# Attention on one core: sums of probabilities moved next to the value products, and one key block more summed by TensorE

## What is computed

```
att   = einsum('bhgqd,bhkd->bhgqk', qg, k) / sqrt(32)
att   = where(causal, att, -inf)
probs = softmax(att, axis=-1)
ctx   = einsum('bhgqk,bhkd->bhgqd', probs, v)
```

## Time and profile before

| | us |
|---|---|
| median of 3 runs | 2504.25 |
| the three runs | 2514.14, 2503.09, 2504.25 |
| span of the profiled execution | 2510.1 |
| that execution's own time: the one run that can contain this span | 2514.14 |
| attention, steady groups 1 to 30 | 664 to 1697 |
| most groups, scores of unit 0 to scores of unit 0 | 33.9 |

### The profile page before, as it was taken

How to read it: one execution, slowest core, us unless ns; L and a number is a source line. 1 busy time by engine, 2 the same in 40 slices (tenths; PEclk the granted TensorE clock), 3 DMA queues, 4 the chain that set the end, 5 groups by cost and what they waited for, 6 DMA issues and landing times. The chain is left out here.

```text
span 2510.1 us, 36950 instructions
## 1 busy us (share of the span) xinstructions
PE 2433.2 (97%) x13716; PEld 1678.6 (67%) x13716; DVE 1698.5 (68%) x2878; ACT 1046.8 (42%) x1873; POOL 1650.9 (66%) x865
## 2 busy tenths in 40 slices
PE   5999999999999999999999999998999999999998
PEld 3788888887555555555555555554688788888886
DVE  4766666677888887888878888873655354455553
ACT  3433333331666666666666666665211111111111
POOL 3743333341798998999989999993755455555543
PEclk9999999999999999999999999999999999999999
DMA  6532333351535325344233334312433333333330
GB/s 229 201 118 85 115 113 116 122 155 72 161 99 145 73 66 160 82 114 108 66 89 82 82 94 137 82 48 93 134 97 96 100 94 101 110 93 100 110 93 25
DMA packets 179727, 267.49 MB, mean 107 GB/s; under 512 B 20508, under 2 KB 113884, under 8 KB 178400
## 3 DMA queue, kind: packets, MB, share of 16 engines
q1 hardware_dynamic: 179552, 265.13, 36.0%
HBM read 183.22 MB, written 80.81 MB: 105 GB/s over the span
## 5 line engine op out<-in xcount | busy, mean ns | idle before, releaser
L1072 POOL TENSOR_TENSOR p_sum<-p_sum,p_ring 128x1024 f32<-128x1024 f32 (+2 forms) x465 | 991.4, 2159 | 81.0 <-PE ctx_ps L1133 59.7
L263 DVE TENSOR_REDUCE neg_max<-scores_q 128x1 f32<-128x512 f32 (+1 forms) x1168 | 708.7, 655 | 124.0 <-PE scores_q L250 66.0
L966 ACT ACTIVATE p_ring<-scores 128x512 f32<-128x512 f32 (+1 forms) x896 | 453.0, 565 | 243.1 <-DVE scores L1020 178.6
L250 PE MATMUL scores_q<-k_stack,q_stack 96*128 96x512 f32 (+1 forms) x1473 | 442.6, 380 | 3.0 <-DVE neg_max L263 2.0
L1112 PE MATMUL scores<-q_stack,k_stack 98*128 98x512 f32 (+1 forms) x1216 | 423.6, 425 | 12.3 <-ACT p_ring L966 8.8
L617 POOL TENSOR_TENSOR roped_hilo<-roped_hilo 128x512 fp32r<-128x512 f32 x80 | 105.8, 1322 | 339.7 <-ACT roped_hilo L459 339.7
L1112 PEld LDWEIGHTS scores<-q_stack,k_stack 98*128 98x128 f32 x1216 | 198.4, 192 | 175.4 <-ACT p_ring L966 93.2
L250 PEld LDWEIGHTS scores_q<-k_stack,q_stack 96*128 96x128 f32 x1473 | 266.2, 192 | 71.2 <-DVE neg_max L263 36.3
L666 PE MATMUL proj_ps<-h_hi,w_hi 128*128 128x512 f32 x752 | 300.3, 399 | 0.7 <-POOL w_lo L606 0.7
L666 PE MATMUL proj_ps<-h_hi,w_lo 128*128 128x512 f32 x752 | 294.3, 391 | 0.0
L666 PE MATMUL proj_ps<-h_lo,w_hi 128*128 128x512 f32 x752 | 293.6, 390 | 0.0
(11 more groups left out here) (178 smaller groups left out, 3709.9 us busy)
## 6 DMA issues: line engine op xcount, KB each, us to landing
q_stack<-qk_t SPq DMA_DIRECT2D x96, 512.0 KB, 6.9
qk_t<-roped_hilo SPq DMA_DIRECT2D x80, 512.0 KB, 2.8
x_in<-in_L_attn_resid SPq DMA_DIRECT2D x32, 512.0 KB, 6.3
ctx_t<-ctx_raw SPq DMA_DIRECT2D x64, 256.0 KB, 5.6
prefetched<-in_L_wmod SPq DMA_DIRECT2D x4, 4096.0 KB, 13.3
prefetched<-ctx_t SPq DMA_DIRECT2D x31, 512.0 KB, 4.1
prefetched<-inv_t SPq DMA_DIRECT2D x124, 128.0 KB, 5.5
k_stack<-qk_t SPq DMA_DIRECT2D x96, 128.0 KB, 8.8
```

What stands on the lines that cost most here:

```text
L250: last = nc.tensor.matmul(dst[:, a, :], qs[0:MHI, h, i * P:(i + 1) * P], ks[0:MHI, lo:lo + w], start=not first and (a == 0 or not diag), s ...
L263: nc.vector.tensor_reduce(sh.negm[:, lo // HALF, hs[0]:hs[-1] + 1, i:i + 1], src, AX.X, ALU.max, negate=True).then_inc(sh.s_mx.sem, 1)
L966: nc.scalar.activation(p[:, a * per:(a + 1) * per, :], src[:, a * per:(a + 1) * per, :], ACT.Exp, scale=SM_SCALE).then_inc(s_ex.sem, 1)
L1072: nc.gpsimd.tensor_tensor(a, a, probs(n, u), ALU.add).then_inc(s_ap.sem, 1)
```

## The change

TAIL_FROM takes unit 18 (key block 6 of the second half) out of GpSimd's list and into the sums product: GpSimd makes 14 additions a group, and the step "sum" of the second half has four more products, of 256 columns each, from the ring. SUM_AT puts the sums of the second half in tick 11 and those of the first in tick 15, where they stand ahead of the value products of the same tick. INV_AT moves the three steps of the inversion from ticks 9, 12 and 15 to 12, 15 and 18. SUM_AT_LAST is as it was.

```diff
-TAIL_FROM = {0: 4, 1: 7}
+TAIL_FROM = {0: 4, 1: 6}
...
-SUM_AT = {1: 9, 0: 16}
+SUM_AT = {1: 11, 0: 15}
 SUM_AT_LAST = {1: 6, 0: 12}
 AHEAD = 5
 TURN_AT = 17
-INV_AT = (9, 12, 15)
+INV_AT = (12, 15, 18)
```

## The result

| | before | after |
|---|---|---|
| median | 2505.1 us (14 runs) | 2511.84 us (14 runs) |
| lowest to highest | 2501.16 to 2514.14 | 2509.37 to 2514.61 |
| ratio of the times | | 1.0024, interval 1.0015 to 1.0032 |
| span of the profiled execution | 2510.1 | 2509.1 (its own time 2510.94) |

The medians differ by 6.7 us, and the ratio puts the cost at 0.24% (0.15 to 0.32%), clear of no change. The forecast from the median was +6 us.

What follows compares the result with a forecast made beforehand. The prediction took TensorE's instruction order as the bound, with two places on VectorE's time, not GpSimd. Terms +7.5 + 4.7 - 2 - 4 = +6 us gave 2510 us from the median 2504.25; range 2494 to 2530.

Steps and rivals of the forecast that it cites:

- sums of the second half with block 6: Ticks 8 to 11: moved sums with four added products cost +0.25 us a group, +7.5 us over 30 groups.
- products of 256 columns: Four products added to the second half's sums on TensorE, eight instructions, 0.43 us by proportion to columns.
- sums of the first half: Moved from tick 16 to 15: mask of tick 17 comes late, +0.15 us a group, +4.7 us over 31.
- inversions: Three reciprocals of 1.74 us on VectorE, moved from tick 12 to VectorE's pause in tick 15: gain 2 us.
- last group: One GpSimd addition less shortens TensorE's 2.82 us wait by 2.4 us and keeps the clock up: -4 us.
- two steady terms: The per-group costs of the moved sums: +7.5 us for the second half, +4.7 us for the first.
- slower: Outcome of a time slower by over 0.5%, chance 0.21: rival A and a small share of the forecast case.
- rival A: VectorE's line in ticks 16 and 17 late by the whole 0.86 us: 22 us more, 2532 us, chance 0.22.
- entry and exit of a burst: Around the second half's 32-column products on TensorE: 0.34 us, paid once and not twice when set ahead of value products.
- the chain by ScalarE's copy and the DMA: From the mask of tick 17 to the next group's first scores: claimed to carry the 0.15 us delay there.
- The claim on the clock: Last group: without the idle time, the stretched eight products keep the 2.4 GHz level, another 2 us gained.
- B: Seams save 0.34 and 0.26 us in full, no bank wait: some -12 us, 2492 us, chance 0.15.

Runs made afterwards that it cites:

- third: Kernel before with block 6 on TensorE, second-half sums in tick 11, inversion later, first-half sums left in tick 16: 2509.4 us, before 2507.61, ratio 1.0.
- seventh experiment: Kernel before with second-half sums in tick 11 and inversion later, block 6 on GpSimd, first-half sums in tick 16: 2499.93 us, before 2508.4, ratio 0.9968.

## Why the prediction was right

| step | forecast, us | from the traces |
|---|---|---|
| sums of the second half with block 6, per group | +0.25 | +0.23 (7.52 to 7.75) |
| of this, products of 256 columns | 0.43 | 0.44 (tick 9, 2.49 to 2.93) |
| sums of the first half, per group | +0.15 | +0.14 (10.96 to 11.10) |
| inversions, together | -2 | -3 (1.0 each: groups 8, 16, 24) |
| last group | -4 | -2.7 |
| groups 0 and 30, beyond these terms | none | +1.4 |
| group 26, a DMA that landed late before | none | -0.6 |
| attention | +6 | +6.2 |

The mechanism of the two steady terms held, and they carry the result: 11.2 us by the traces, 12.2 forecast. That the total agrees to a fraction of a microsecond is luck in part. The inversions gave 1 us more than forecast and the last group 1.3 us less, and groups 0, 26 and 30, which the forecast left out, add 0.8 us. The chances have a small slip: "slower" got 0.21, less than the 0.22 of rival A alone.

*The bound.* That GpSimd at 93% busy was no bound is shown twice: 2.38 us less a group gave nothing, and 0.65 us more on TensorE cost 0.63. The Trainium skill's rule (Perfetto Trace Analysis, Identifying the Most-Contended Engine), by which the engine of the highest occupancy is the one to optimize, would have ranked the relief of GpSimd as a gain. In this kernel the measurement decides against it, although with one small addition more the same engine does become the bound in some groups.

*The second half.* The working held to 0.02 us: entry and exit of a burst of products with 32 output rows cost 0.34 us once, and the sums start 2.30 us after the scores of tick 10 (992.14 to 994.44), where 2.14 is the way without a wait: 0.16 us of waiting for the bank, 0.17 forecast.

*The first half.* The size was right and half of its reason wrong. The mask of tick 17 is late (1007.38 is 2.10 us after the scores of tick 16, as forecast), and VectorE's line carries that on. But the prediction let the chain by ScalarE's copy and the DMA carry it to the next group. With the turn a tick earlier that chain is free, and the period stays; by the rows it is the banks that carry it.

*The inversions* were undersized. The forecast took TensorE's one visible wait of 0.85 us and left 0.15 of cost. The three groups in fact had 1.0 us more than their neighbours before and none after (34.24 to 34.27). With the sums in tick 15 too, the reciprocal fits wholly into the pause under the longer burst; with the sums in tick 16 (third and seventh experiment) these groups keep 0.2 us.

*The last group.* The wait for GpSimd of 2.82 us is gone, as forecast. The claim on the clock was wrong as it stood: without that wait the half-clock stretch didn't vanish, it moved. Two windows of the last group after, in which the third number from the end of a row is the granted clock:

```profile
1703.00:1707.00 4.00, 3.96 (x23) 2.28 (x24) 0.87 (x2) 2.39 (x5) 4.00 (x3) 0.57 0.00 0
...
1728.00:1732.00 4.00, 4.00 (x28) 1.02 (x32) 0.42 (x1) 1.17 (x3) 0.00 (x0) 0.68 0.00 0
```

The first follows a wait of 1.85 us for the DMA of the maxima, the second several waits for exponentials, and the value products of tick 15 took 1.6 us longer. Ticks 6 and 7, where the wait had been, gained 5.1 us; ticks 0 and 1 lost 1.4 and tick 15 lost 1.6 at the lower clock. So the last group gained 2.7 us and not 4.

*Groups 0, 26 and 30.* Group 0 has no sums of the second half, so by the forecast's terms it grows by 0.15 us; it grew by 0.9. The rest is in tick 5, which over the fourteen traces takes 0.1 to 1.6 us more than in other groups; in the four kernels with the second half in tick 11, block 6 on GpSimd and the first half in tick 16 or later it takes 0.1, 0.4, 1.0 and 1.0 us more, although they are the same up to there. So it can be scatter; its cause wasn't looked into. Group 26 took 34.45 us before, 0.56 more than its neighbours, all of it in tick 19, and 34.27 after. Group 30 grew by 0.65 us beyond the period's growth. In both TensorE waits for a DMA of the maxima's rows that landed late, see the last section. GpSimd's load isn't what makes group 26 long: with even more work on GpSimd (unit 19 given back to it) that group takes the 33.65 us of its neighbours. So no place in the steady part is shown where the lighter GpSimd pays.

*What the profile would show.* 14 additions a group, 34.3 us a period, 2.1 us to the mask of tick 17, 3 us of pause for VectorE: as foretold. GpSimd's pause at tick 11 is 2.97 us and not 3.8, as it now runs ahead far enough to wait for ScalarE too (1.26 us at 986.57). Neither rival A nor B came in.

*A reading that didn't hold.* The profiled execution of before was taken for the run of 2514.14 us, since only that one could contain the span. In all later runs the time is 1.8 us above the span; by that the profiled one took some 2512 us and was none of the three. The forecast stood on the median and isn't touched.

## What to carry to other kernels

An engine that is busy 93% of the time is no bound while it waits once a round for another. Read the size of that wait, and its distance to the point where its result is needed, before work is taken off it or given to it. Work moved to the engine whose order sets the period is paid by the column, while a move within that order can be free or even pay, if it saves a seam and doesn't take a neighbour's cover away: here one of the two moves gained 0.20 us a group, the other lost 0.14. Undo such changes part by part: the version with the good move and the later inversion is 0.3% faster than the kernel before, and so beats both.

## What the hardware showed that I hadn't expected

The half-clock stretches of the last group don't go away with the longest wait. Before there was one of 6.8 us in it. After there are stretches at other places, and in the run with block 6 alone a drop comes 5.8 us into the group, although TensorE doesn't wait for GpSimd there. The other way round, the version with the second half moved keeps a wait of 2.85 us for GpSimd in its last group, as long as the 2.82 us before, and its granted clock is 1.00 over the whole group (1689 to 1722 us). So this wait alone doesn't decide on the clock.

The DMA of the maxima's rows goes out in two parts. In group 30 these landed 2.8 us (median of the two) after their issue in four traces (the changed kernel, block 6 alone, the first half left, and the sums in tick 18) and 2.1 us after it in the kernel before and the nine others. The last tick of group 30 took 4.0 to 4.7 us in the first three of these, against 3.3 in the traces with 2.1 and the turn in tick 17 as before, but for one (3.7). It doesn't go with block 6 on TensorE: the fourth has that block on GpSimd, and the kernels with blocks 5 and 6 on TensorE and with the turn in tick 16 show 2.1 us.

What it goes with are loads of instructions, DMAs of 8 or 16 KB in queues of their own. Group 26 of the kernel before, 1560 to 1563.6 us, and of the changed kernel, 1564.2 to 1567.4 us (only the first has the load):

```profile
q8 instruction: 1, 0.02, 2.4%
...
q_stack<-neg_max_rows SPq DMA_DIRECT2D x2, 16.0 KB, 2.6
```

```profile
q_stack<-neg_max_rows SPq DMA_DIRECT2D x2, 16.0 KB, 2.1
```

The fourteen traces have 434 such DMAs. Of the 277 with no instruction load in their time, none lands over 0.05 us later than usual. 69 land more than 0.1 us late, and each has a load in its time. In 24 a load of 16 KB begins 0.4 to 2.15 us after the first issue, and all of these are late, by 0.45 to 1.9 us; among them are group 30 in the four traces above and group 26 in eight. Loads that begin earlier or later often delay nothing. That the load is the cause is argued from this coincidence; no run moved a load by itself. It is a reason not to read a microsecond in one group of one trace as the work of the change.
